# Two transformer layers on one core: the second layer's first attention placed beside the first layer's last per-token steps

## The reference, cut to what matters

```
x = x + tanh(g_xattn[0]) * attn0(layernorm(x), ctx)     # 16 heads of 64, causal
x = x + tanh(g_ffn[0])   * ffn0(layernorm(x))           # per token: attention among 16 heads, then 8 gated experts
x = x + tanh(g_xattn[1]) * attn1(layernorm(x), ctx)     # 16 heads of 16, not causal
x = x + tanh(g_ffn[1])   * ffn1(layernorm(x))           # 3 x (256 -> 1024 -> 256), one of two routed plus one shared
```

## Time and profile before

| | us |
|---|---|
| median of 3 runs (2657.82 to 2660.02) | 2659.93 |
| the profiled execution's own time | 2663.2 |
| its span, first to last instruction | 2661.4 |
| PE busy | 2325.5 (87%) |
| DVE busy | 1487.3 (56%) |
| ACT busy | 1268.0 (48%) |
| POOL busy | 1019.5 (38%) |

### The profile page before, as it was taken

One profiled execution on the slowest core, in us unless ns is written; L12 is line 12 of the kernel. 1 busy time (PEld: TensorE's weight loads), 2 busy tenths in 40 slices (PEclk: granted clock), 3 DMA queues, 4 the chain that ended last, 5 costly groups with the idle time before them and its releaser, 6 DMA issues. The chain is left out here.

```text
span 2661.4 us, 48220 instructions
## 1 busy us (share of the span) xinstructions
PE 2325.5 (87%) x16128; PEld 1931.7 (73%) x16128; DVE 1487.3 (56%) x3906; ACT 1268.0 (48%) x3971; POOL 1019.5 (38%) x910
## 2 busy tenths in 40 slices
PE   5888989888888898888466999999999999999998
PEld 4667777777777777776354777877777887777777
DVE  3467667666766676767635445444444544444441
ACT  5655566555556555556023444433344443334441
POOL 1355554555554455555512333222233322223320
PEclk9989999999999999999667999999999999999999
DMA  4000000000000000000040000000000000000000
GB/s 145 14 6 17 13 16 4 16 16 16 16 12 4 16 16 16 16 4 9 4 161 1 13 17 16 16 16 16 4 12 16 16 16 16 16 4 12 16 9 9
DMA packets 25856, 51.66 MB, mean 19 GB/s; under 512 B 6272, under 2 KB 7040, under 8 KB 24640
## 3 DMA queue, kind: packets, MB, share of 16 engines
q1 hardware_dynamic: 25792, 50.84, 5.7%
HBM read 42.44 MB, written 8.39 MB: 19 GB/s over the span
## 5 line engine op out<-in xcount | busy, mean ns | idle before, releaser
L1191 POOL TENSOR_SCALAR l_probs<-l_probs,l_rinv 128x256 f32<-128x256 f32 x512 | 238.4, 480 | 590.0 <-DVE l_rinv L1406 589.4
L1302 ACT ACTIVATE l_probs<-l_score,l_negmax 128x256 f32<-128x256 f32 x512 | 238.4, 472 | 265.0 <-DVE l_negmax L1401 265.0
L364 POOL TENSOR_TENSOR l_prod<-l_att,l_kv 128x2048 f32<-128x2048 f32 x64 | 287.4, 4527 | 180.7 <-DVE l_att L637 180.7
L350 POOL TENSOR_TENSOR l_prod<-l_q,l_kv 128x2048 f32<-128x2048 f32 x64 | 290.3, 4547 | 155.9 <-DVE l_att L620 84.1
L1606 PE MATMUL l_ffn<-l_w,l_hid 128*128 128x256 f32 x1536 | 347.9, 382 | 1.0 <-ACT l_hid L1276 1.0
L1606 PEld LDWEIGHTS l_ffn<-l_w,l_hid 128*128 128x128 f32 x1536 | 287.6, 190 | 51.0 <-issue 14.3
L1413 DVE COPY l_probsT<-l_attn 128x512 f32<-128x512 f32 x256 | 175.5, 685 | 161.1 <-PE l_attn L1569 160.9
L710 DVE CUSTOM_DVE_ANT_0 l_probs<-l_score,l_mbias 128x256 f32<-128x256 f32 (+1 forms) x512 | 161.3, 353 | 147.5 <-PE l_score L906 97.6
L1401 DVE TENSOR_REDUCE l_negmax<-l_score 128x2 f32<-128x512 f32 x256 | 175.1, 684 | 65.4 <-PE l_score L1557 65.4
L643 DVE TENSOR_REDUCE l_h<-l_prod 128x128 f32<-128x2048 f32 x64 | 146.3, 2286 | 110.7 <-POOL l_prod L364 110.7
L439 ACT ACTIVATE l_probs<-l_probs,l_negmax 128x256 f32<-128x256 f32 x256 | 130.8, 511 | 107.7 <-DVE l_negmax L710 106.5
(11 more groups left out here) (271 smaller groups left out, 7527.2 us busy)
## 6 DMA issues: line engine op xcount, KB each, us to landing
l_ctxin<-in_ctx SPq DMA_DIRECT2D x32, 256.0 KB, 3.0
l_xin<-in_x SPq DMA_DIRECT2D x16, 256.0 KB, 2.7
l_x<-in_x SPq DMA_DIRECT2D x16, 256.0 KB, 2.6
x<-l_acc SPq DMA_DIRECT2D x16, 256.0 KB, 2.0
l_xin<-x SPq DMA_DIRECT2D x16, 256.0 KB, 3.3
l_x<-x SPq DMA_DIRECT2D x16, 256.0 KB, 2.6
out<-l_x SPq DMA_DIRECT2D x16, 256.0 KB, 2.0
l_hid<-in_w SPq DMA_DIRECT2D x2, 1536.0 KB, 8.6
```

The lines of the kernel that those rows point to most:

```text
L350: nc.gpsimd.tensor_tensor(prod[:, u].rearrange("p (h g d) -> p h g d", h=half, g=H), q4[:, u * half:(u + 1) * half].unsqueeze(2).to_broadc ...
L364: nc.gpsimd.tensor_tensor(prod[:, u].rearrange("p (h d g) -> p h d g", h=half, d=HD), a4.unsqueeze(2).to_broadcast([P, half, HD, H]), v4.u ...
L1191: last = nc.gpsimd.tensor_scalar(probs[:, j % 4, t * S:(t + 1) * S], probs[:, j % 4, t * S:(t + 1) * S], rinv[:, j, t:t + 1], 1.0, ALU.mul ...
L1302: last = nc.scalar.activation(probs[:, s % 4, t * S:(t + 1) * S], ps[:, t * S:(t + 1) * S], ACT.Exp, bias=negmax[:, s, t:t + 1], accum_out ...
```

## The change

The two blocks become one. Each engine's program of either layer becomes a generator that yields its place, a number in steps of the last layer-0 turn with attention: `body(15, 14, 13, None)` has places 0 to 20, `body(None, 15, 14, None)` has `TAIL + s` (TAIL is 21), `body(None, None, 15, None)` has `2 * TAIL + s / 2`. Layer 1's loads and splits stand at places 6 to 15, its element-0 projections at 20.2 and 20.6, `body(0, None, 1)` at `TAIL + s`, `body(1, 0, 2)` at `2 * TAIL + s`. `side_by_side` writes, on each engine, always the piece with the lowest place next; at a tie the first layer's goes first.

Memory is allocated in two stacks. "Left" holds layer 0's attention (and layer 1's weights and attention), "right" holds layer 0's mix and experts (and layer 1's w1, w2 and feed-forward). Layer 1's attention starts when x1 of element 15 is ready; w1 and w2 can only be loaded when x2 of element 15 is stored. So layer 1's first feed-forward is late: `begin(0)` and the two w1 splits stand at step 13 of `body(1, 0, 2)` (`FFN_LATE` is 14), h0 to h11 come two a step at steps 14 to 19, and y0 and y1 both follow the attention's output. Layer 1 no longer makes its own identity, constants and tanh, and loads no second copy of the gates.

```
+def side_by_side(*programs):
+    ahead = [(next(p), n, p) for n, p in enumerate(programs)]
+    while ahead:
+        _, n, p = ahead.pop(ahead.index(min(ahead)))
+        at = next(p, None)
+        if at is not None:
+            ahead.append((at, n, p))
...
 # layer 0, gpsimd body
+                yield 5.5
                 query_key(b, 0, 0)
+                yield 6.5
                 query_key(b, 0, 1)
+                yield 8.5
                 query_key(b, 1, 0)
+                yield 9.5
                 query_key(b, 1, 1)
                 for piece in range(4):
+                    yield 13.5 + piece
                     weigh(b, piece)
...
 # layer 0, end of each engine's program
+        for s in body(B - 1, B - 2, B - 3, None):
+            yield s
+        for s in body(None, B - 1, B - 2, None):
+            yield TAIL + s
+        for s in body(None, None, B - 1, None):
+            yield 2 * TAIL + s / 2
...
 # layer 1, sync
+        yield 6
+        _, full, _, turn = past.attn.at("q3", B - 1)
+        sp.wait_ge(full, turn)
         load(0)
+        for n in range(NS_FIRST):
...
+        load(1)
+        yield TAIL + BEGIN
+        sp.wait_ge(past.x1_ready, B)
         load_residual(0)
...
+        yield TAIL + STEPS
+        load(2)
+        yield 3 * TAIL
+        sp.wait_ge(past.x2_stored, 16 * B)
+        for n in range(NS_FIRST, NS):
+            sp.dma_start(raw(n), splits[n][0]).then_inc(raw_in[n % 2], 16)
         sp.dma_start(flat(w2), ins["w2"]).then_inc(w2_in, 16)
         load_residual(1)
+        store(0)
+        load_residual(2)
+        with sp.Fori(3, B) as b:
...
 # layer 1, scalar body (vector and tensor alike)
+                if first(b) and s == FFN_LATE - 1:
+                    for n in range(NS_FIRST, NS):
+                        split(n)
+                    begin(b)
+                if first(b) and s == FFN_LATE:
+                    act.wait_ge(split_lo, NS)
+                if b is not None:
+                    for j in up_at(b, s):
+                        hidden(b, j)
...
+    def up_at(b, s):
+        if first(b):
+            return (2 * (s - FFN_LATE), 2 * (s - FFN_LATE) + 1) if s >= FFN_LATE else ()
+        return (s,) if s < 12 else ()
...
+            @block.tensor
+            def _(pe):
+                side_by_side(one.tensor(pe), two.tensor(pe))
```

More of the change, by code:

```diff
@@ L8 @@
+from collections import namedtuple
 from contextlib import ExitStack
@@ L249, in layer0, with network @@
+def network(nc, ins, x2, out):
+    with ExitStack() as both:
+        with ExitStack() as left, ExitStack() as right:
+            one, past = layer0(nc, ins, x2, left, right, both)
+        with ExitStack() as left, ExitStack() as right:
+            two = layer1(nc, ins, x2, out, left, right, both, past)
         with nc.Block() as block:
@@ L289, in _ @@
-                load(2)
-                load_residual(1)
-                with sp.Fori(3, B) as b:
-                    load(b)
-                    load_residual(b - 1)
-                    store(b - 3)
-                load_residual(B - 1)
-                for b in (B - 3, B - 2, B - 1):
-                    store(b)
-                sp.wait_ge(x2_stored, 16 * B)
+                side_by_side(one.sync(sp), two.sync(sp))
             @block.gpsimd
             def _(pool):
-                nc.gpsimd.memset(ident[:], 0.0)
@@ L412, in _ @@
-                for k in range(NS_FIRST):
-                    split(k)
-                act.wait_ge(params_in, 16 * len(params))
-                nc.scalar.activation(tg[:], gates[:], ACT.Tanh).then_inc(tanh_done, 1)
-                def high(banks, use, batch, dst, ready, scales=None):
-                    ps, full, free, turn = banks.at(use, batch)
-                    act.wait_ge(full, turn)
-                    if scales is None:
-                        nc.scalar.copy(dst[:].rearrange("p c n -> p (c n)"), ps[:]).then_inc(ready, 1)
-                    else:
-                        for c in range(ND):
-                            last = nc.scalar.activation(dst[:, c, :], ps[:, c * S:(c + 1) * S], ACT.Copy, scale=scales[:, c:c + 1])
-                        last.then_inc(ready, 1)
@@ L532, in _ @@
-                for use in attn.ahead:
-                    project(use, 0)
-                body(0, None, None, 1)
-                body(1, 0, None, 2)
-                body(2, 1, 0, 3)
-                with act.Fori(3, B - 1) as a:
-                    body(a, a - 1, a - 2, a + 1)
-                body(B - 1, B - 2, B - 3, None)
-                body(None, B - 1, B - 2, None)
-                body(None, None, B - 1, None)
+                side_by_side(one.scalar(act), two.scalar(act))
             @block.vector
@@ L544, in _ @@
             def _(dve):
-                for banks in (attn, score, heads, side):
-                    banks.open(dve)
-                V = nc.vector
-                def variance(src, stat, mv, var, ready):
-                    for t in range(NT):
-                        V.bn_stats(stat[:, t], src[:, t])
-                    dve.drain()
-                    for t in range(NT):
-                        V.bn_aggr(mv[:, t], stat[:, t])
-                    dve.drain()
-                    V.tensor_scalar(var[:], mv[:, :, 1], LN_EPS, None, ALU.add).then_inc(ready, 1)
@@ L811, in _ @@
-                pre_variance(0)
-                split(0)
-                pre_normalise(0)
-                for k in range(1, NS_FIRST):
-                    split(k)
-                dve.wait_ge(params_in, 16 * len(params))
-                dve.wait_ge(tanh_done, 1)
-                low(attn, "xT", 0, xT, xT_hi)
-                body(0, None, None, 1)
-                body(1, 0, None, 2)
-                body(2, 1, 0, 3)
-                with dve.Fori(3, B - 1) as a:
-                    body(a, a - 1, a - 2, a + 1)
@@ L824, in _ @@
-                body(B - 1, B - 2, B - 3, None)
-                body(None, B - 1, B - 2, None)
-                body(None, None, B - 1, None)
+                side_by_side(one.vector(dve), two.vector(dve))
             @block.tensor
             def _(pe):
-                T = nc.tensor
-                def transpose4(banks, use, batch, src):
-                    ps, full, free, turn = banks.at(use, batch)
-                    pe.wait_ge(free, turn)
-                    for c in range(ND):
-                        for t in range(NT):
-                            last = T.transpose(ps[:, c * S + t * P:c * S + (t + 1) * P], src[:, t, c * P:(c + 1) * P], ident[:])
-                    last.then_inc(full, 1)
```

2626 lines of the change are left out of this document (1381 added, 1245 removed).

## The result

The changed kernel takes 2638.0 us (median of 4 runs, 2631.7 to 2640.4), the kernel before, beside it, 2658.9 (2657.1 to 2660.0): ratio 0.9918, 95% interval 0.9900 to 0.9937. I had predicted 2608 with a range of 2574 to 2642. The direction was right and the time lies in the range, but the gain is 21 us where I forecast 52.

What follows compares the result with a forecast made beforehand. It took PE to bound the loops, no engine to be full in the changed stretch, and VectorE to become fullest in B. 3 + 93.4 + 3 + 109 = 208.4 against 260.5 us: 52 less, 2608 us, eight in ten 2574 to 2642.

Steps and rivals of the forecast that it cites:

- A: Layer 1's preparation beside body(15, 14, 13, None), x1(14) to x1(15): adds 3 us, bounds 0 and 7.1.
- B: body(None, 15, 14, None) merged with body(0, None, 1), x1(15) to x3(0): 93.4 us, VectorE's work plus idle; bounds 80 and 105.
- the 105: Upper bound in us for the merged stretch from x1(15); passing it was to show the prediction wrong.
- I count 3.15 ... and nothing for the second: In B, VectorE's normalisation of element 1 collides with a GpSimd product, the queries' combination does not: 3 us added.
- the bound of 9: Upper bound in us for VectorE's waits on GpSimd's products in B: two whole pieces.
- GpSimd's order: In B, head normalisations queue behind 4.5 us product pieces; that delay fits before the transpositions, so nothing was added.
- C: body(None, None, 15, None) beside body(1, 0, 2), from x3(0), with late feed-forward and y0: 109 us, bounds 98 and 125.
- The loops: All code before and after the changed stretch is the same in the same order: no cost.
- R2: Rival, chance 0.17: head pairs run in series with layer 0's pieces; B 108, C 121, 28 us less, 2632.
- R1: Rival, chance 0.22: B runs at layer 0's own pace, 80 us, with C at 100; 77 us less, 2583.
- R3: Rival, chance 0.04: in-order queues let nothing overlap, so the chains add; 4 us slower, 2661.
- R4: Rival, chance 0.07: layer 1's projections or loads come late, so B starts late; gain 30 us, 2630.

Runs made afterwards that it cites:

- a_bq: Changed kernel with only layer 1's scaling of bq moved from place 15 to 19.5 on VectorE: 2632.3 us.
- a_end: Changed kernel with the first split kept at place 11 and layer 1's other VectorE preparation moved to 19.5, behind the last product: 2628.1 us.
- amp_scalar: Changed kernel plus two small tensor_scalar instructions per layer-0 loop turn on VectorE, beside GpSimd's weighing pieces: 2684.2 us.
- amp_reduce: Changed kernel plus two small tensor_reduce instructions per layer-0 loop turn on VectorE, beside GpSimd's weighing pieces: 2640.2 us.
- best2: a_end with the second and third splits moved on into B, where VectorE waits for ScalarE: 2626.7 us.
- x_all: Changed kernel with calculation left out in B on VectorE (reductions), GpSimd (products) and TensorE (expert matmuls) together: 2623.4 us.
- single cuts: Changed kernel with calculation left out in B on one engine: VectorE's reductions 2635.0 us, GpSimd's products 2633.8, TensorE's expert matmuls 2636.4.
- a_all: Changed kernel with mean, normalisation and first two splits moved to place 12.5, third split and bq scaling to 19.5: 2629.0 us.
- start_late: Changed kernel with layer 1's first projections moved behind layer 0's output product at the start of B: 2638.1 us.
- b_pace: Changed kernel with layer 0's places in body(None, 15, 14, None) multiplied by 0.8 on every engine: 2642.8 us.
- b_act: Changed kernel with all 16 normalisations of layer 1's first attention moved from GpSimd to ScalarE: 2645.9 us.
- b_tail: best2 with the normalisations of heads 12 to 15 of layer 1's first attention moved from GpSimd to ScalarE: 2627.4 us.
- c_first: Changed kernel with x3 of element 1 computed ahead of the sum of y0 of element 0 on VectorE: 2637.6 us.

## Why the prediction was off, step by step

- **A, "Bounds: 0, all hidden ... and 7.1 ... I take 3"**: this is the step that failed: the term was 3 and measured 16.9. Two things went wrong in it. I knew the collision of the earlier trace rows and applied it in B alone, while A puts tensor_scalar and two-input instructions of VectorE beside the same eight products. And I let VectorE's 21.4 us of idle time hide the work, though part of it stands ahead of the softmax's division, behind which GpSimd's 18 us of weighing end the turn. Shown: 89.9 to 82.2 by the place of one instruction (a_bq), to 78.4 by order alone, with all of the work still in A (a_end), so 11.5 of the 16.9 are order; that the form of the instruction and the product beside it make the delay is shown by amp_scalar and amp_reduce. TensorE's granted clock in A, 0.96 before and 0.81 in the changed kernel, came back to 0.93 (a_end) and 0.94 (best2) by order alone, so it fell with the delays; its part in the 11.5 isn't separated. What is left, 5.4, and 4.2 with two splits moved on to B (best2), is VectorE's work where nothing hides it, near the 3 that I took.
- **B, "72.0 + 21.4 = 93.4"**: this step failed second, by 9.3, and B passed the 105 that I had set as a sign of being wrong. The work was right (73.9 us of VectorE with the collision, 56.9 of GpSimd where I had 56.4, 29.2 of ScalarE where I had 30; TensorE's 75.7 at a clock of 0.81 are 61 at full clock where I had 57). The idle time taken from layer 0's turn was too small, 31.8 for 21.4. x_all shows that it hardly shrinks (30.5) when 11.4 us of VectorE's busy time, 17.1 of GpSimd's and 10.1 of PE's go; and the single cuts, that no one engine's work stands behind it. Nor did any of six other orders give a B under 101.8. I had read the idle time as a property of the kind of turn. That it belongs to the hand-overs of this pair of streams fits all four cuts and is argued from them; which hand-overs, one by one, stays open.
- **"I count 3.15 ... and nothing for the second"**: the other way round. The normalisation in B took 1.07 (two instructions, 0.73 by themselves) and the combination of q 3.08. The sum, 2.7 (3.2 with the mean, 0.68 for 0.17), agrees with the 3, by luck; for the bound of 9 was nearly reached in a_all, start_late, b_pace, amp_scalar and amp_reduce, with 7.5 to 7.7 us of holding each. For a merge of this kind the 9 was as good a value as the 3. The Trainium skill, "SBUF — State Buffer", section "SBUF: two separate sides", says that the pair of ports is locked for a whole instruction, by VectorE's two-port modes and by its instructions with two SBUF inputs. The runs agree: a combination with two SBUF inputs took 3.08 for 0.75, and of the amplifiers the tensor_scalar had a median of 2.27 us, the tensor_reduce of 0.145. Whether a tensor_scalar here runs in a two-port mode, no row shows. The 8.40 shows besides that GpSimd can get the next turn as well.
- **GpSimd's order, "4.5 us of delay fits; I add nothing"**: right in the main, not wholly. TensorE did wait for normalisations, 4.1 us in B; moving them to ScalarE cost more (b_act, b_tail).
- **C, 109**: right to 2.6. Step 13 at +55.2 (+54), the stand for the splits as forecast in kind, with no wait before ScalarE for w1 (the first cast began at 1443.33, right behind its exponentials) and 12.3 us from step 13 to step 14 where I had 10.5; y0 seen ahead of x3(1) instead of behind it, without effect (c_first). The upper bound of 18.5 for the stand put all three splits behind the second half of w1; as only the second half's two need it, the same rows give 15 (63 + 2.75 + 3.36 - 54). The 3 for the low clock behind the stand is about what was paid: 44.1 us at a mean of 0.94, which is 2.6 short of full clock (an estimate, with TensorE busy for 43.1).
- **The loops, "I cost that at nothing"**: 0.2 us a turn in layer 1, 1.7 in all; not explained.
- **The rivals**: R2's number, 2632, is nearest to the result, but in part by luck: it had A at 3 where 16.9 was measured, and C at 121 with w1 late, where C was 111.6 and w1 came in time. Its B, 108, is nearer to 105.7 than mine. Its reason for it, the two score banks, no run tests; TensorE's waits for exponentials in B come to 6.1 us. R1, R3 and R4 are out: B wasn't 80, the chains didn't add up, and layer 1's first projection in B was through VectorE 4.5 us after x1(15).

best2 beats both kernels: 0.9880 (0.9860 to 0.9900), 31.5 us less than the kernel before in its own rounds (2658.2). Its median is 11.3 below the changed kernel's, and its slowest execution (2631.5) is just below the changed kernel's fastest (2631.7).

## What to carry to other kernels

Before work is put beside a long GpSimd product, sort VectorE's instructions in that stretch by form: each tensor_scalar between SBUF tiles and each instruction with two SBUF inputs can cost the rest of the product beside it, and at times the next one, however small it is, and its place in the order is worth more than its size. In A, VectorE's idle time could take work only where nothing that ends the turn was queued behind it, so ask of each gap what starts after it. And where two chains are merged, take the idle part of the sum as uncertain by half: here it was 31.8 us for 21.4, and cutting any engine's work gave back only a third to a half of the cut.

## What the runs showed that I had not expected

- A scaling of two numbers per partition took up to 6.7 us (amp_scalar) and a combination of 0.75 us took 8.40 in four of the kernels, through two products of GpSimd with normalisations between them. In the changed kernel and five others it got through behind the first product, 3.01 to 3.08 us, and there GpSimd's normalisation took 1.40 instead of 0.93. It isn't the moment at which q arrives: in all ten it began 2.0 to 2.1 us into GpSimd's third piece. What decides between the two is open.
- It works the other way too: two pieces of weighing took 9.97 us (from 1248.20), as VectorE's split of 1.2 us ran between them, where two pieces of the earlier trace rows took 8.98.
- The reciprocal of 128x2 and the tensor_reduces, SBUF to SBUF, ran at their usual 0.15 and 2.29 us beside products.
